# Attention and feed-forward kernel: reading both PSUM banks of every turned tile on ScalarE instead of one bank each on ScalarE and VectorE

## What is computed

```
h1 = ln(x);  x = attn(h1, h1, wq, wk, wv, wo) + x         # 16 heads of 32
h2 = ln(x);  x = attn(h2, context, ...) + x
attn: q, k, v = h@wq, c@wk, c@wv
      sim  = fq(q) @ fq(k).T * scale;  p = softmax(sim)
      out  = fq(p, 8 bits, zp 0) @ fq(v);  return out @ wo + bo
fq(x) = (clip(round(x/delta) + zp, 0, 255) - zp) * delta
```

## Time and profile before

| | |
|---|---|
| median of 3 runs | 3019.38 us (3018.3 to 3019.39) |
| the profiled execution | 3019.96 us |
| its span, first to last instruction | 3018.2 us |
| busy in the span: PE, DVE, ACT, POOL | 93%, 59%, 48%, 23% |
| mean granted clock of PE | 0.968 |
| the quantised stage | 0 to 1228 us |

### The profile page before, as it was taken

One profiled execution on the slowest core, in us unless ns is written; L12 is line 12 of the kernel. 1 busy time (PEld: TensorE's weight loads), 2 busy tenths in 40 slices (PEclk: granted clock), 3 DMA queues, 4 the chain that ended last, 5 costly groups with the idle time before them and its releaser, 6 DMA issues. The chain is left out here.

```text
span 3018.2 us, 54146 instructions
## 1 busy us (share of the span) xinstructions
PE 2806.9 (93%) x17920; PEld 2214.6 (73%) x17920; DVE 1771.2 (59%) x4484; ACT 1455.2 (48%) x3763; POOL 692.1 (23%) x1147
## 2 busy tenths in 40 slices
PE   5799999999999996699999997999999999999997
PEld 5566666666666663599999996888888888888885
DVE  6799899999999986433333335344444444444432
ACT  4577777777777765211111112444444444444442
POOL 1222222222222221133333322112111111111110
PEclk8899999999999997799999998999999999999997
DMA  4443343333333342400010004000000000000000
GB/s 144 83 82 80 80 85 85 79 84 85 83 80 80 87 77 54 152 29 28 28 42 28 28 21 140 22 28 35 28 28 28 28 28 28 28 28 28 35 15 14
DMA packets 325753, 169.11 MB, mean 56 GB/s; under 512 B 274240, under 2 KB 290624, under 8 KB 325696
## 3 DMA queue, kind: packets, MB, share of 16 engines
q1 hardware_dynamic: 325696, 168.39, 22.0%
HBM read 76.07 MB, written 25.17 MB: 34 GB/s over the span
## 5 line engine op out<-in xcount | busy, mean ns | idle before, releaser
L595 ACT ACTIVATE e<-S,bias,qk_scale 128x256 f32<-128x256 f32 x1024 | 563.6, 564 | 65.3 <-DVE e L707 61.4
L690 DVE TENSOR_REDUCE negmax<-S 128x4 f32<-128x1024 f32 x256 | 312.0, 1219 | 105.3 <-PE S L503 103.7
L707 DVE TENSOR_SCALAR e<-e,rsum 128x256 f16<-128x256 f32 x1024 | 291.8, 348 | 2.5
L565 ACT ACTIVATE shifted<-PJ,round_col,inv 128x512 f32<-128x512 f32 x192 | 149.4, 778 | 227.5 <-PE PJ L157 226.5
L1584 POOL TENSOR_TENSOR mid_partsB<-mid_actB,mid_partsB 128x256 fp32r<-128x256 f32 x128 | 102.1, 797 | 611.8 <-DVE mid_partsB L1482 611.8
L148 PE MATMUL PJ<-w_a_wo,oT 128*128 128x512 f32 x512 | 239.6, 612 | 2.6 <-ACT oT L604 1.8
L157 PE MATMUL PJ<-hT,w_a_wq 128*128 128x256 f32 x1536 | 208.3, 294 | 21.5 <-DVE hT L685 17.7
L157 PEld LDWEIGHTS PJ<-hT,w_a_wq 128*128 128x128 f32 x1536 | 195.4, 199 | 35.5 <-issue 35.5
L595 ACT ACTIVATION_READ_ACCUMULATOR e<-S,bias,qk_scale 128x1 f32 x1024 | 209.1, 204 | 0.0
L157 PE MATMUL AG0A<-h_partsA,upA 128*128 128x256 f32 x1536 | 200.0, 287 | 7.2 <-POOL h_partsA L1579 3.4
L157 PE MATMUL AG0B<-h_partsB,upB 128*128 128x256 f32 x1536 | 199.1, 286 | 7.6 <-POOL h_partsB L1579 6.4
(11 more groups left out here) (186 smaller groups left out, 5578.8 us busy)
## 6 DMA issues: line engine op xcount, KB each, us to landing
x_in<-in_x_dram SPq DMA_DIRECT2D x16, 512.0 KB, 3.5
ctx_in<-in_ctx_dram SPq DMA_DIRECT2D x16, 512.0 KB, 3.5
mid_dram<-x SPq DMA_DIRECT2D x16, 512.0 KB, 2.7
y_inA<-mid_dram SPq DMA_DIRECT2D x16, 512.0 KB, 3.6
part_dram<-x3A SPq DMA_DIRECT2D x16, 512.0 KB, 4.0
y_inB<-mid_dram SPq DMA_DIRECT2D x16, 512.0 KB, 3.2
kv_in<-in_ctx_dram SPq DMA_DIRECT2D x16, 512.0 KB, 4.7
baseB<-part_dram SPq DMA_DIRECT2D x16, 512.0 KB, 3.2
```

The source lines that it names most:

```text
L565: nc.scalar.activation(shifted[:, bank, :], PJ[bank][:], ACT.Identity, bias=round_col[:, 0:1], scale=inv[:, d:d + 1]).then_inc(pj_emptied[ ...
L595: nc.scalar.activation(e[:, s, i, :], S[s][:, i // 2, i % 2, :], ACT.Exp, bias=bias[:, s, i:i + 1], scale=qk_scale[:, ph.a:ph.a + 1], accu ...
L690: nc.vector.tensor_reduce(negmax[:, g % 2, :], S[g % 2][:].rearrange("p i q n -> p (i q) n"), AX_X, ALU.max, negate=True).then_inc(max_don ...
L707: nc.vector.tensor_scalar(e16[:, s, i, :], e[:, s, i, :], rsum[:, s, i:i + 1], ROUND16, ALU.mult, ALU.add).then_inc(prob_scaled, 1)
```

## The change

ACT now takes both banks of every turned tile out of PSUM, one after the other, each behind its own `pj_filled` wait. DVE no longer waits for bank 1 to be filled and no longer reads it; its `wait_emptied` for bank 1, which stood there before, is now the wait for ACT. The high part of ACT's half comes after both reads. Nothing else is changed.

```diff
@@ act_transposed
-                if kind_of(name) == "ctxT":
-                    nc.scalar.copy(turned[:, 0:2, :], PJ[0][:].rearrange("p (c n) -> p c n", c=2)).then_inc(
-                        pj_emptied[0], 1)
-                else:
-                    i = "2" if kind_of(name) == "h2T" else "1"
-                    affine_act(turned, PJ[0], 0, cols[f"ln{i}_g"], cols[f"ln{i}_b"], pj_emptied[0])
+                for bank in range(2):
+                    wait_filled(act, (stage, b, name, bank))
+                    if kind_of(name) == "ctxT":
+                        nc.scalar.copy(turned[:, 2 * bank:2 * bank + 2, :],
+                                       PJ[bank][:].rearrange("p (c n) -> p c n", c=2)).then_inc(pj_emptied[bank], 1)
+                    else:
+                        i = "2" if kind_of(name) == "h2T" else "1"
+                        affine_act(turned, PJ[bank], bank, cols[f"ln{i}_g"], cols[f"ln{i}_b"], pj_emptied[bank])
                 wait_emptied(act, where)
                 nc.scalar.copy(parts_of(where)[:, 0, 0:2, :], turned[:, 0:2, :]).then_inc(turned_high_done, 1)
@@ dve_transposed
-                wait_filled(dve, where)
-                if kind_of(name) == "ctxT":
-                    nc.vector.tensor_copy(turned[:, 2:4, :], PJ[1][:].rearrange("p (c n) -> p c n", c=2)).then_inc(
-                        pj_emptied[1], 1)
-                else:
-                    i = "2" if kind_of(name) == "h2T" else "1"
-                    affine_dve(turned, PJ[1], 1, cols[f"ln{i}_g"], cols[f"ln{i}_b"], pj_emptied[1])
                 wait_emptied(dve, where)
                 parts = parts_of(where)
                 nc.vector.tensor_copy(parts[:, 0, 2:4, :], turned[:, 2:4, :]).then_inc(turned_high_done, 1)
```

## The result

The changed kernel takes **3040.99 us** (median of 4 runs, 3040.14 to 3043.72) against 3018.84 for the kernel before beside it (4 runs, 3018.18 to 3019.39): ratio 1.0072, with a 95% interval of 1.0057 to 1.0087. It is 0.7% slower; the forecast was 3038.5. The profiled execution took 3041.38 us, with a span of 3039.4.

The account below looks back on a forecast made before the run. PE was taken as the bound, with short handovers. `hT` 8.3, clock with one `h2T` cost 9.8 and ends 1.1 summed to 19.2 us on 3019.96, 3039.2; the median, 0.6 lower, gave 3038.5 us, range 3029 to 3047.

Parts of the forecast that it names:

- PE is the bound: In the quantised stage's thirteen rounds PE, busy 94%, sets the time, with short handovers the same in each round.
- the `xhat` chain: PE's 1.98 us wait for DVE's `xhat` is a chain PE to DVE to PE without the removed work.
- `hT`, 0.60 us a round: Group 7: ACT empties bank 1 later, so `v2`,1 starts 0.60 us later; thirteen rounds plus 0.5 ahead make 8.3 us.
- hidden, with 0.3 to spare: At `hT`, ACT's exponentials end 0.8 us later, about 561.3, still ahead of the scores at about 561.6.
- `h2T`, 0.6 us with the full clock: Group 0: scores wait 0.49 us for ACT's exponentials, DVE's work comes 0.6 later; 0.6 us a full-clock round, otherwise hidden.
- `ctxT`, nothing: Group 4: bank 1 is empty at about 508.95 and PE needs it only behind the scores at 512.21; cost 0.
- the cover that I named: At `ctxT`, exponentials 0.4 us later end near 511.7, ahead of scores at 512.21; without that cover 0.4 a round.
- The clock, 9.8 us with one 0.6 in it: Slow 1.2 GHz stretches: five more behind `h2T`, two behind `hT`, at 1.31 us each, plus one `h2T` cost of 0.6.
- at `h2T` nothing gets shorter: PE's waits around `h2T` don't shrink, so five of the six fast rounds were taken to become slow.
- The ends, +1.1: Outside the repeating rounds: +0.7 at `hT@0`, +0.4 at the last `ctxT`, +0.5 at the last `h2T`, -0.5 at `hT@1`.
- the -0.5 that I took: At `hT@1` DVE, late to its pair, no longer has one to do: -0.5 us, bounds -1 and +0.7.
- DVE was the bound after all: Rival, 5%: the chain to `xhat` shortens as DVE's backlog does, at most 26 us less 8 at `hT`: 3001 us.

Follow-up runs that it names:

- run 4: Kernel before, but DVE copies only one column of each half of bank 1, leaving out needed work: 3013.33 us, ratio 0.9982.
- run 1: Kernel before, with ACT taking both banks at `hT` alone, `h2T` and `ctxT` as before: 3030.99 us, ratio 1.0033.
- run 5: Changed kernel, but ACT reads bank 1 ahead of bank 0 at `hT`: 3044.00 us, ratio 1.0086.
- run 3: Kernel before, with ACT taking both banks at `ctxT` alone: 3020.70 us, ratio 1.0003.
- run 12: Changed kernel, with DVE making `xhat` ahead of the probabilities in group 7 of a round's first phase: 3022.89 us, ratio 1.0009.
- run 11: Kernel before, with DVE making `xhat` ahead of the probabilities in group 7 of a round's first phase: 3043.16 us, ratio 1.0073.
- run 2: Kernel before, with ACT taking both banks at `h2T` alone, `hT` and `ctxT` as before: 3026.92 us, ratio 1.0017.
- run 10: Changed kernel, but DVE does the last group's probabilities ahead of the turned tile's parts: 3033.12 us, ratio 1.0038.
- run 7: Changed kernel, but DVE makes the high part of both halves in one instruction and ACT none: 3046.34 us, ratio 1.0090.
- run 9: Changed kernel, with PE filling and ACT reading bank 1 first at `hT`, ACT not waiting for bank 0 beforehand: 3029.32 us, ratio 1.0028.

## Why the prediction was right, point by point

- **PE is the bound, and the `xhat` chain holds no turned work.** Right, and shown: the wait reads 27.8 us in 14 places before, after and in run 4.
- **`hT`, 0.60 us a round.** The mechanism was right and shown from both sides: run 1 alone gives C to B 40.35, and freeing the bank in run 4 brings `v2`,1 forward by 0.83 us. It also bounds the finding: a later bank costs its full time, but one that comes 0.83 earlier gives only 0.13, since ACT's exponentials and the DMA then end last. The size was 0.70. `v2`,1 waits 1.40 where 1.36 was worked out, from four affines of 1.93 where 1.94 was taken, and the remaining few hundredths lie behind it. The exponentials I had "hidden, with 0.3 to spare" were so: no score wait stands behind `v2`,1. That margin is thin, as run 5 shows.
- **`h2T`, 0.6 us with the full clock.** 0.69: a score wait of 0.42 (worked out 0.49) and a DMA wait of 0.20 behind it. In rounds with a fall it is hidden but for some 0.05, as said.
- **`ctxT`, nothing.** Within 0.1 us a round, run 3. It was not quite the cover that I named: ACT's exponentials do come late for the scores, and the `xhat` wait takes up half.
- **The clock, 9.8 us with one 0.6 in it.** This is the term that came out right by its total and not by its parts. I took five more falls behind `h2T` and two behind `hT`, seven in all at 1.31. There were two and four, six in all, the latter at 1.48; and four rounds, not one, paid the full price at `h2T`. That the totals agree (9.2 us forecast, 8.5 measured) is luck. The step that failed is "at `h2T` nothing gets shorter", from which I let nearly all rounds fall there. In the kernel before the six fast rounds had the same waits of 1.98 and 0.5 us as the seven slow ones, so the waits alone could not say which would turn slow. Runs 1 and 12 show how far the falls move with small shifts of the order. Why a round has one here and none there I can't derive from these traces; that stays open. The Trainium skill, "TensorE: Matmul & The Clock Gate", A second HAM failure mode: psum-queue depth-cycling, names short idles between groups of matmuls as a cause of such swings; the traces agree in so far as in both kernels each fall comes behind two such idles (0.72 and 1.40 us at the `hT` above), but the idles do not decide it: the same 0.72 and 1.40 stand at all thirteen `hT` places of run 1, with a granted clock of 1.00 behind each.
- **The ends, +1.1.** Wrong in sign for the part before the loop. At `hT@0` PE starts 1.0 later (25.96 against 24.95; I had 0.7), but the product there runs 7.31 us instead of 8.56 and gives it back; the granted clock reads 1.00 in both, and no run explains it. At `hT@1` the gain was 1.04 (51.56 against 52.60), the lower bound and not the -0.5 that I took. The loop begins at 174.69 instead of 175.94. Behind the loop, up to the first transposes of stage two, 0.2 us is added, although the waits at the last `ctxT` (3.28 against 2.85) and the last `h2T` (3.27 against 2.64) grew as forecast; the last 1.5 us of the 21.2 lie in stages that the change doesn't touch, and no run explains them.
- **DVE was the bound after all.** False for this order of the work. Runs 11 and 12 give its condition: once `xhat` is moved ahead of the probabilities, DVE's queue is on PE's path, and its relief does pay.
- **DVE is busy 37 us less in the loop.** It was 34.5: the 37 adds up single instructions (0.535 us each), but a pair on DVE is busy for 0.99 us.

The sum was 19.2 us and the profiled executions differ by 21.4: handovers 8.9 forecast (0.5 of it ahead of the loop), 11.8 measured in the loop; clock 9.2, 8.5; ends 1.1, about 0.5; loose ends in the loop 0.5.

## What to carry to other kernels

Here work taken off an engine that is busy 91% of the time was worth nothing, and giving it to the other party of the same handover made PE wait longer; read who ends the wait last, and add the burst's length, not its work, to that place. After a move, follow the receiving engine's next products (here ACT's exponentials) and the relieving engine's new waits, since an engine in order spends what it was freed of standing for its supplier. And where the granted clock falls in some rounds and not in others, as here, carry the clock as a term of its own with wide bounds: it was worth 8.5 us beside 11.8 of handovers, and between runs 11 and 12 more than they.

## What the runs showed that was not expected

**The clock's falls have no rule that these runs give.** Over the thirteen rounds of the loop, by the granted clock of each stretch:

| | round without a fall, us | rounds with a fall | behind `h2T` | behind `hT` |
|---|---|---|---|---|
| before | 69.29 | 7 | 7 | 0 |
| changed | 70.67 | 13 | 9 | 4 |
| run 1 (`hT` alone) | 70.00 | 11 | 11 | 0 |
| run 2 (`h2T` alone) | 69.98 | 11 | 11 | 1 |
| run 3 (`ctxT` alone) | 69.33 | 7 | 7 | 0 |
| run 10 | 70.31 | 10 | 8 | 2 |
| run 11 | 70.28 | 10 | 8 | 2 |
| run 12 | 69.92 | 2 | 0 | 2 |

Most rounds have one fall or none, but not all: the first round of run 2 and the eleventh of run 7 have one behind each of the two places. Before and after the change a fall is a piece of 3.4 us at about 0.5 and costs 1.31 us behind `h2T` and 1.48 behind `hT`. That price belongs to these orders of the work: in run 9 a stretch from `h2T` to `hT` with a fall is 0.23 to 0.74 us longer than the shortest without. The cheap ones are those in which the clock is down already in the transposes (1.89 us instead of 1.09 for those at 246.29), and PE then has no wait for the bank behind them.

**DVE's probabilities at double length.** With `xhat` early, the four conversions of one group take 2.15 us where others take 1.14; both lines are of run 11, on DVE:

```profile
531.00 2.15 DVE L707 TENSOR_SCALAR e<-e,rsum 128x256 f16<-128x256 f32 x4
...
537.87 1.14 DVE L707 TENSOR_SCALAR e<-e,rsum 128x256 f16<-128x256 f32 x4
```

and on POOL in the same run:

```profile
530.86 1.35 POOL L806 TENSOR_TENSOR x_bo<-x_in,rows 128x512 f32<-128x512 f32 x1
```

One of the four is the long one: it takes 1.36 us by itself, from 531.00 on, where the median is 0.35, and ends 0.15 us behind POOL's addition. That addition of two SBUF tensors runs beside the conversions of just one group in each of the thirteen rounds, and these thirteen are the ones that take 2.1 us, while the other 183 take 1.1; in the kernel before it lies beside a maximum that reads PSUM, at 526.11, which keeps its 1.21 us. The same 2.15 stands at 525.79 of run 12 with POOL's addition at 525.64. That the two block each other is inferred from this overlap; no run took the addition away. The Trainium skill, "SBUF — State Buffer", SBUF: two separate sides, says that DVE and GpSimd take a shared pair of ports as an exclusive lock, the one that starts first holding it for its whole instruction; on DVE's side this is for an instruction in a two-port mode or with two SBUF inputs, and no run here shows which mode the conversion runs in. The 1.01 us that the trace shows is less than POOL's 1.35, so it fits a conversion held back until the addition ended. My forecasts of runs 11 and 12 lacked this microsecond; how much of the two misses it makes was not measured.
